# Linear-attention kernel, two layers: k's softmax chain in pieces, k'v's sums in another PSUM bank, q dealt by two engines, one output tile ahead of k'v

## The reference, cut to what matters

```
xn = layernorm(x)
q, k, v = xn @ Wq + bq, xn @ Wk + bk, xn @ Wv + bv      # k and v masked
q = softmax(q of a head, over its columns)
k = softmax(k of a head, over the 512 tokens)
att = einsum(k, v)            # per head, k'v
y = einsum(q, att)
scale, shift = silu(emb) @ W_emb + b_emb
h = layernorm(y) * (1 + scale) + shift
x = x + silu(h) @ W_out + b_out
```

## Time and profile before

| | us |
|---|---|
| median of 3 runs | 852.2 (851.95 to 852.74) |
| the profiled execution | 852.96 |
| its span | 851.2 |
| its granted TensorE clock, mean | 0.99 |
| TensorE busy | 788.6 (93%) |
| VectorE busy | 610.0 (72%) |
| ScalarE busy | 443.5 (52%) |
| GpSimd busy | 387.4 (46%) |
| DMA queue of SyncE | 42.8% of 16 engines |

### The profile page before, as it was taken

One profiled execution on the slowest core, in us unless ns is written; L12 is line 12 of the kernel. 1 busy time (PEld: TensorE's weight loads), 2 busy tenths in 40 slices (PEclk: granted clock), 3 DMA queues, 4 the chain that ended last, 5 costly groups with the idle time before them and its releaser, 6 DMA issues.

```text
span 851.2 us, 15057 instructions
## 1 busy us (share of the span) xinstructions
PE 788.6 (93%) x5307; PEld 681.6 (80%) x5307; DVE 610.0 (72%) x1277; ACT 443.5 (52%) x660; POOL 387.4 (46%) x444
## 2 busy tenths in 40 slices
PE   7987969998999999899999989999898999989997
PEld 6656758887888888788888878888787888878886
DVE  6777858768685876868587686857768685764664
ACT  6341383646547263664846366472646637273642
POOL 3040243626455262656746266452625445352462
PEclk9998979999999999999999999999999999999999
DMA  8972234343434434345483434344243434426112
GB/s 264 320 244 66 87 94 149 78 148 115 134 134 136 148 78 151 113 133 183 119 267 96 149 113 143 135 133 156 72 130 135 124 135 114 131 65 233 33 68 99
DMA packets 121687, 115.36 MB, mean 136 GB/s; under 512 B 16152, under 2 KB 106264, under 8 KB 115744
## 3 DMA queue, kind: packets, MB, share of 16 engines
q1 hardware_dynamic: 121632, 114.65, 42.8%
HBM read 51.68 MB, written 16.78 MB: 80 GB/s over the span
## 4 chain that ended last, share of the span: by engine, by line
PE 74%; DVE 17%; issue 4%; ACT 1%; SPq 1%; POOL 1%; DMA 1%; DVEq 0%; POOLq 0%; ACTq 0%
PE psum_w L489 43%; PE psum_k L489 20%; PE psum_t L581 6%; DVE q L974 3%; PE psum_k L720 3%; DVE k_top L944 2%; DVE y L987 1%; DVE k_shift_rows L962 1%; DVE y_stats L994 1%; DVE k_top L941 1%; DVE k_top L950 1%; SPq L389 1%; DVE q_max L976 1%; DVE y_moments L998 1%; DVE k_exp L801 1%
## 5 line engine op out<-in xcount | busy, mean ns | idle before, releaser
L1461 POOL TENSOR_TENSOR q<-q,q_max 128x512 f32<-128x512 f32 x64 | 67.1, 1048 | 244.6 <-DVE q_max L976 244.6
L1284 ACT ACTIVATE q<-q 128x512 f32<-128x512 f32 x64 | 40.1, 626 | 235.9 <-POOL q L1461 235.9
L489 PE MATMUL psum_w<-w_high_v,xT_high 128*128 128x512 f32 x240 | 93.0, 387 | 22.1 <-DVE q L974 22.1
L1413 POOL TENSOR_TENSOR gT_low<-yT,gT_high 128x512 fp32r<-128x512 f32 x56 | 71.8, 1285 | 69.9 <-ACT gT_high L1254 66.7
L489 PE MATMUL psum_k<-w_high_k,xT_high 128*128 128x512 f32 x240 | 93.6, 390 | 8.6 <-DVE att L1042 6.5
L1405 POOL TENSOR_TENSOR xT_low<-xT,xT_high 128x512 fp32r<-128x512 f32 x56 | 71.7, 1281 | 57.1 <-ACT xT_high L1208 53.5
L489 PE MATMUL psum_w<-w_high_q,xT_high 128*128 128x512 f32 x240 | 94.9, 395 | 0.0
L489 PE MATMUL psum_w<-w_high_o,gT_high 128*128 128x512 f32 x240 | 92.6, 386 | 0.0
L489 PE MATMUL psum_k<-w_low_k,xT_high 128*128 128x512 f32 x240 | 92.2, 384 | 0.0
L489 PE MATMUL psum_k<-w_high_k,xT_low 128*128 128x512 f32 x240 | 92.0, 383 | 0.0
L489 PE MATMUL psum_w<-w_low_v,xT_high 128*128 128x512 f32 x240 | 91.0, 379 | 0.0
(11 more groups left out here) (189 smaller groups left out, 1840.9 us busy)
## 6 DMA issues: line engine op xcount, KB each, us to landing
qT<-k_exp SPq DMA_DIRECT2D x240, 64.0 KB, 2.0
yT<-raw_weights SPq DMA_DIRECT2D x240, 64.0 KB, 2.0
xT<-raw_weights SPq DMA_DIRECT2D x224, 64.0 KB, 2.0
raw_weights<-x_between_layers SPq DMA_DIRECT2D x10, 1024.0 KB, 6.9
x_res<-in_x SPq DMA_DIRECT2D x8, 1024.0 KB, 5.0
x_between_layers<-x_res SPq DMA_DIRECT2D x8, 1024.0 KB, 4.1
raw_weights<-in_x SPq DMA_DIRECT2D x6, 1024.0 KB, 6.7
x_res<-x_between_layers SPq DMA_DIRECT2D x6, 1024.0 KB, 4.8
```

The source lines that it names most:

```text
L489: mm = pe.matmul(bank, lhs[:, c, of_tile(t)], alternating(rhs[m][:, c, :]), start=(c == 0 and n == 0), stop=(c == CHUNKS - 1 and n == 2))
L1284: act.activation(q[:, t, :], q[:, t, :], ACT.Exp).then_inc(q_exp_ready, 1)
L1413: pool.tensor_tensor(low[:, c, :], yT[:, c, :], high[:, c, :], ALU.subtract).then_inc(g_low_ready, 1)
L1461: pool.tensor_tensor(rows_q, rows_q, q_max[:, t, 0:HEADS[layer]].unsqueeze(2) .to_broadcast([P, HEADS[layer], width]), ALU.subtract).then_ ...
```

## The change

PSUM: k'v's sums go to `psum_t` bank 0, in iteration 0 to `psum_w` bank 0; K tile 0 waits for no `att_ready`, k'v waits until y of the batch before is taken.

```diff
-        def att_psum_of(layer):
-            return head_view(psum_k[:, 0, :], layer, SUMS)
+        def att_psum_of(i, layer):
+            bank = psum_w[:, 0, :] if fixed(i, 0) else psum_t[:, 0, :, :].rearrange("p c n -> p (c n)")
+            return head_view(bank, layer, SUMS)
```

```diff
                     if t == 0:
-                        pe.wait_ge(att_ready, i)
...
-                    if t >= 2:
-                        attend(i - 1, t - 2, att_layer)
+                    if t >= 1:
+                        attend(i - 1, t - 1, att_layer)
...
                     project(i, t, Q, psum_w[:, t % 2, :])
-                    if t < 2:
-                        attend(i - 1, t + 2, att_layer)
+                    if t == 0:
+                        attend(i - 1, 3, att_layer)
...
+                if gives_out(i):
+                    out_projection(i - 2, 0, v_ready, TILES * i + 3)
                 pe.wait_ge(k_exp_ready, TILES * (i + 1))
                 pe.wait_ge(v_ready, TILES * (i + 1))
                 pe.wait_ge(v_masks_ready, 2 * (i + 1))
+                if fixed(i, 0):
+                    pe.wait_ge(q_biased, 3)
+                elif fixed(i, LAST):
+                    pe.wait_ge(qT_ready, 3)
+                else:
+                    wait_apart(pe, y_ready, TILES * i)
```

VectorE: `k_shift_of` is cut into `k_top_of_halves` (L937 to L946), `k_top_of_all` (L947 to L953) and `spread_k_shift` (L954 to L963), `shift_k` takes two tiles at a time, and y is normalised here. The old order is L1099 to L1147; the new one:

```diff
+                raise_k_max(i, 0)
+                if turns_x: turn_x_blocks(i + 1, 0); turn_x_blocks(i + 1, 1)
+                raise_k_max(i, 1)
+                take_y(j, att_layer, 0)
+                if turns_x: turn_x_blocks(i + 1, 2)
+                stats_of_y(j, 0)
+                raise_k_max(i, 2)
+                take_y(j, att_layer, 1)
+                if turns_x: turn_x_blocks(i + 1, 3)
+                stats_of_y(j, 1)
+                if turns_x_late: turn_x_blocks(i + 1, t) for all t     # iteration 1
+                raise_k_max(i, 3); turn_k_max(i)
+                take_y(j, att_layer, 2); k_top_of_halves(i)
+                take_q(i, layer, 0);     k_top_of_all(i)
+                take_y(j, att_layer, 3)
+                take_q(i, layer, 1);     spread_k_shift(i, layer)
+                take_q(i, layer, 2);     shift_k(i, (0, 1))
+                take_q(i, layer, 3);     shift_k(i, (2, 3))
+                stats_of_y(j, 2); stats_of_y(j, 3)
+                moments_of_y(j, t) for all t
+                if normalises_x(i): x_stats_of(i + 2)
+                for t in range(TILES):
+                    normalise_y(j, t)
+                    turn_y_blocks(j, t)
+                if gives_out(i) and not fixed(i, LAST): add_residual(i - 2, 0)
+                turn_q_blocks(i, t) for all t
                 sum_attention(i, layer)
...
+            def normalise_y(j, t):
+                if t == 0:
+                    dve.wait_ge(y_factors_done, 2 * (j + 1))
+                dve.tensor_scalar(y[:, t, :], y[:, t, :], y_moments[:, t, 0:1], y_rstd[:, t:t + 1],
+                                  ALU.subtract, ALU.mult).then_inc(yn_ready, 1)
```

ScalarE loses `normalise_y`; exp of q tile 3 goes behind exp of k tiles 0 and 1; in iteration 1 `prepare_x(2)` goes between the masks of v; and it issues eight of q's DMAs, SyncE the other eight:

```diff
+        def deal_q(eng, i, quadrants):
+            eng.wait_ge(q_blocked, TILES * (i + 1))
+            if attends(i):
+                wait_apart(eng, y_psum, TILES * i)
+            deal(eng, qT[:, :, :, :].rearrange("p a c n -> p a (c n)"), q_blocks, q_dealt, quadrants)
...
+                    deal_q(sp, i, (2, 3))
...
                     normalise_x(i + 2)
...
+                if not fixed(i, LAST):
+                    deal_q(act, i, (0, 1))
                 act.wait_ge(table_loaded, i + 1)
                 preload_silu()
```

GpSimd: y's factors need two instructions in place of four, and the order, of all iterations, is:

```diff
-                shift_q(i, layer, 0)
-                shift_q(i, layer, 1)
+                for t in range(TILES):
+                    shift_q(i, layer, t)
+                if gives_out(i):
+                    bias_residual(i - 2, 0)
+                    bias_residual(i - 2, 1)
                 if attends(i):
                     y_factors(i - 1)
-                shift_q(i, layer, 2)
-                shift_q(i, layer, 3)
                 if gives_out(i):
-                    for t in range(TILES):
-                        bias_residual(i - 2, t)
+                    bias_residual(i - 2, 2)
+                    bias_residual(i - 2, 3)
+                if normalises_x(i):
+                    x_factors(i + 2)
                 if not fixed(i, LAST):
                     low_of_x(i + 1)
-                if normalises_x(i):
-                    x_factors(i + 2)
```

More of the change, by code:

```diff
@@ L919, in raise_k_max @@
             def raise_k_max(i, t):
+                if t == 0 and attends(i):
+                    wait_apart(dve, att_ready, i)
                 dve.wait_ge(k_psum, TILES * i + t + 1)
@@ L933, in turn_k_max, with k_top_of_halves @@
                 dve.transpose(k_turned[:, :, :].rearrange("p b r -> p (b r)"), k_max[:, :]).then_inc(k_max_turned, 1)
-            def k_shift_of(i, layer):
-                of_quad, other_half, of_half, other_quad, of_all, shift = (k_top[:, n, :] for n in range(6))
+            of_quad, other_half, of_half, other_quad, of_all, shift = (k_top[:, n, :] for n in range(6))
+            def k_top_of_halves(i):
                 steps = K_TOP_STEPS * i
@@ L1098, in iteration @@
                 j = i - 1
+                turns_x, turns_x_late = deals_x(i) and not fixed(i, 1), fixed(i, 1)
                 raise_k_max(i, 0)
-                if deals_x(i):
+                if turns_x:
                     turn_x_blocks(i + 1, 0)
@@ L1123, in iteration @@
                     moments_of_y(j, t)
-                take_q(i, layer, 2)
-                k_shift_of(i, layer)
-                take_q(i, layer, 3)
-                for t in range(TILES):
-                    turn_y_blocks(j, t)
-                shift_k(i)
                 if normalises_x(i):
                     x_stats_of(i + 2)
+                for t in range(TILES):
+                    normalise_y(j, t)
+                    turn_y_blocks(j, t)
+                if gives_out(i) and not fixed(i, LAST):
+                    add_residual(i - 2, 0)
                 if not fixed(i, LAST):
@@ L1134, in iteration @@
                         turn_q_blocks(i, t)
-                if gives_out(i) and not fixed(i, LAST):
-                    add_residual(i - 2, 0)
                 sum_attention(i, layer)
@@ L1289, in copy_last_q @@
                          psum_t[:, t % 2, :, :].rearrange("p c s -> p (c s)")).then_inc(qT_ready, 1)
-            def normalise_y(j):
-                act.wait_ge(y_factors_done, 4 * (j + 1))
-                for t in range(TILES):
-                    act.activation(y[:, t, :], y[:, t, :], ACT.Identity, scale=y_rstd[:, t:t + 1],
-                                   bias=y_offset[:, t:t + 1]).then_inc(y_normed, 1)
             def normalise_x(i):
@@ L1349, in iteration @@
                     copy_last_q(2)
[L1350 to L1351 removed]
+                if fixed(i, 1):
+                    prepare_x(2, 0, (2,))
                 mask_v(i, layer, 3)
@@ L1354, in iteration @@
                     copy_last_q(3)
+                elif fixed(i, 1):
+                    prepare_x(2, 0, (3,))
                 else:
```

130 lines of the change are left out of this document (70 added, 60 removed).

## The result

The changed kernel takes 829.6 us (median of 4 runs, 827.62 to 830.04), the kernel before beside it 852.5: a ratio of 0.972, 95% interval 0.970 to 0.975. The profiled execution took 827.62 with a span of 825.8, the fastest of the four; before it was 852.96 and 851.2. So the two traces differ by 25.4 us, the medians by 22.9. In what follows every number of one kernel is from its one profiled execution, and medians are named.

What follows compares the result with a forecast made beforehand. TensorE was taken to set the time, its waiting to be what can be won. Middle -33.9, start -0.5 and end +4.0 sum to -30.4 us: 821.8 against the median of 852.2, range 812 to 835.

Steps and rivals of the forecast that it cites:

- the likeliest case: The forecast itself, whole kernel: 821.8 us, own range 816 to 828, chance 0.61.
- The middle: End of iteration 2's attends to K tile 0 of iteration 15: 39.1 us of waits and restarts fall to 5.2, -33.9.
- The chain in pieces: k's shift chain on VectorE, split between takes of y and q: V tile 1's wait goes, 1.6 us to spare.
- output tile 0: Put ahead of k'v on TensorE: its 2.59 us cover V tile 3's mask and exp of k; k'v's wait goes.
- VectorE's late stretch: VectorE's work after q tile 3, through y's normalisations and transposes: ends at 38.5, before k'v's end at 39.1.
- The normalisation: y's normalisation, moved to VectorE after x's statistics: 1.0 us each, bounds 0.45 and 1.3.
- the first rival: VectorE's late stretch replaces the wait; output tile 3 or A1 waits 0.5 to 1.2 us per iteration: 834 us, chance 0.18.
- the third rival: DMA issues of ScalarE and SyncE slow each other, y's deal ends 5.1 us later: 867 us, chance 0.06.
- The loop in it: y's landing, A1, Q3, y's transposes, next landing: 45.7 us, hidden under TensorE's 46.9; 50.8 if the deal is stretched.
- The start: Up to attend 3 and Q1 of iteration 2: ends at about 139.7 for 140.2, -0.5 us, between -4 and +4.
- The end: From K tile 0 of iteration 15: y's transposes end later, delaying the last gate and add; +4.0 us, between 1 and 6.
- The -1.0 and +0.6: Terms of the end: 1.0 us off for GpSimd's former waits for VectorE, 0.6 added for lower clock after a wait.

Runs made afterwards that it cites:

- the kernel before with this part alone: Against the kernel before: exp(q)'s transfers dealt by two engines, ScalarE tiles 0 and 1, SyncE tiles 2 and 3; 857.7 us, ratio 1.007.

## Why the prediction was right or wrong

The forecast was 821.8 and the result 829.6: inside the range of 812 to 835, outside the 816 to 828 of the likeliest case. In the terms of the profiled executions 30.4 us less were forecast, and 25.3 were found. Of the other 2.7 us, 2.0 are that the profiled run after was the fastest of its four, and 0.7 that the one before stood that much above its median.

**The middle: -33.9 forecast, -34.4 found.** The chain in pieces and output tile 0 work as forecast: undone they cost 19.2 and 12.7 us of the twelve iterations, and output tile 0 with its add gives 10.6 when done alone. Undoing the new bank or the normalisation on VectorE costs the middle 3.5 and 4.2, little above the spread, and leaves the steady periods within 0.1 us of the changed kernel's. The size is right by luck: two errors cancel. I kept 0.4 us an iteration for slips; there are none, and the periods are 46.47 and 47.25, exactly the work (16 products, four attends and k'v). That is 5 us better. Against it iterations 7 and 8, the change of layers, take 97.3 for 93.7, which I did not look at; no row of mine was from there. (Rows of the kernel before would not have shown it: its iterations 7 and 8 take 49.4 and 50.0, as their neighbours.) There GpSimd makes the low part of weights beside k's chain. Of the changed kernel, GpSimd's timeline in iteration 7 and VectorE's:

```profile
369.09 4.98 POOL L1466 TENSOR_TENSOR w_low_k<-raw_weights,w_high_k 128x512 fp32r<-128x512 f32 x4 [1.74 <-ACT w_high_k L1227]
```

```profile
371.67 1.20 DVE L964 COPY k_top<-k_top 64x16 f32<-64x16 f32 x1
372.90 1.20 DVE L966 TENSOR_TENSOR k_top<-k_top 128x16 f32<-128x16 f32 x1
```

**The account of the three parts was incomplete.** I gave output tile 0 no other condition than its own bank's. That its add had to go ahead of q's transposes is in the diff, and I took it for a detail; without it three quarters of this part are lost (2.8 for 10.6). The same add is missing from the sum for VectorE's late stretch: it takes 0.65 us between y's last transpose, forecast for 38.5, and k'v's end at 39.1, so that the cover of 0.6 was none by my own numbers.

**The normalisation: 1.0 us taken, 0.80 measured** (60 of them, from 0.50 to 1.6). The one at 341.78 takes 1.26 beside a GpSimd instruction on the residual's bias, two later ones 0.51. y's transposes end at 38.0 for 38.5. That the normalisations are shorter than assumed, 0.8 us for the four, makes up for the add that I left out: VectorE is through 0.16 ahead of k'v's end. So the first rival was close, and that it did not come true is in part luck.

**Two issuers: the third rival was wrong.** The median issue takes 0.63 us on ScalarE (0.60 to 1.18) and 0.60 on SyncE (0.59 to 1.85), which is SyncE's median in the kernel before too; the median landing is 2.0 to 2.1 us on both. The loop in it was right in kind, and it is what the kernel with all of q on SyncE falls into. That ScalarE would have 27% of the span to spare is a slip: 443.5 us busy and 15 times 5.1 of 851.2 leave 39%. Nothing hung on it.

**The start: -0.5 forecast, +2.7 found.** The mechanism I named came as forecast: GpSimd's low part at 69.4 (69.2), K tile 0 at 71.1 (70.5). What failed is the term for iteration 2. y's deal landed 2 us later than my 124.5, and I had put no price on the clock behind attend 1's wait. The changed kernel's windows of 129 to 132 and 132 to 136 (busy of PE, PEld, DVE, ACT, POOL, then clock, DMA share, GB/s):

```profile
129.00:132.00 3.00, 2.56 (x10) 2.50 (x11) 2.57 (x6) 2.94 (x5) 2.80 (x3) 0.50 0.33 85
132.00:136.00 4.00, 4.00 (x14) 3.27 (x14) 1.80 (x4) 1.29 (x2) 1.27 (x1) 0.62 0.17 44
```

Attend 1 takes 2.10 - 1.06 = 1.0 us more than one at full clock, K tile 3 there 4.38 for 2.59. The start also spreads: K tile 0 of iteration 1 was at 71.1 to 73.0 in the seven kernels whose iteration 0 is nearly or wholly that of the changed one, and at 65.2 to 67.0 in the four of the old kind. The two traces that I compare are the earliest of either kind, so the 3.2 us that separate forecast and trace are uncertain by 2 us either way.

**The end: +4.0 forecast, +6.4 found.** The path is the forecast one, and the term mis-sized is the 4.4 for y's transposes: they end 37.7 after K tile 0 (36.1), 6.1 later than before. The forecast let the factors wait for two `bias_residual`, but named no time for the factors themselves. They take 1.3 us (767.66 to 769.01 on GpSimd), and VectorE waits until then. The -1.0 and +0.6 I can't tell apart in the trace. This is VectorE's first normalisation in iteration 15, and SyncE's deal behind it:

```profile
769.04 1.50 DVE L809 TENSOR_SCALAR y<-y,y_moments,y_rstd 128x512 f32<-128x512 f32 x1 [2.24 <-POOL y_rstd L1435]
```

```profile
775.10 10.71 SPq L331 DMA_DIRECT2D yT<-raw_weights  x16
```

GpSimd's queue holds the first normalisation of the last batch, too:

```profile
796.30 1.48 DVE L1074 TENSOR_SCALAR y<-y,y_moments,y_rstd 128x512 f32<-128x512 f32 x1 [8.69 <-POOL y_rstd L1514]
```

**The marks** that I had named: no wait of V tile 1 (none; in iteration 7 0.85 ahead of a Q tile and 0.34 ahead of V tile 0), k'v right behind output tile 0 (yes), periods 46.9 and 47.5 (46.5 and 47.25), `low_of_x(1)` near 69 (yes), the last y 4.4 later (6.1).

## What to carry to other kernels

When a wait is taken out by doing work earlier, follow the buffer that this work fills to whoever must empty it: the wait returns there if its reader stands behind an unrelated wait. A chain of transfers through one issuer is a loop; compare its period with the work's before shortening anything else. Price the first and the last iteration by themselves: here a change that gained 34 us in the middle lost 9 at the two ends, and mending those, by order and by one more deal on two engines, gave 20 by the medians and 15 by the traces.

## What was not expected of the hardware

The text at the start says that each engine runs its instructions in the program's order. ScalarE's DMA issues did not wait for the arithmetic ahead of them in its program. In iteration 6 its first q transfer is issued at 350.90 while three of four x normalisations, which come first in the program, begin later. From the changed kernel's timeline of ScalarE:

```profile
350.45 0.81 ACT L1336 ACTIVATE raw_weights<-raw_weights,x_offset,x_rstd 128x512 f32<-128x512 f32 x1
350.90 0.61 ACTq L331 DMA_DIRECT2D qT<-k_exp  x1
351.17 0.80 ACT L1336 ACTIVATE raw_weights<-raw_weights,x_offset,x_rstd 128x512 f32<-128x512 f32 x1
351.54 0.62 ACTq L331 DMA_DIRECT2D qT<-k_exp  x1
```

I had q's issues begin 44.0 us after K tile 0; they begin at 41.4. The other way round they did wait. In the kernel before with this part alone, the cast that follows eight issues starts only as the last is out (68.94), and in every iteration of the changed kernel but the last, which has no such issues, ScalarE's table load starts only behind the last of them (356.43 in iteration 6, after 3.06 us idle). So in these traces arithmetic waits for issues ahead of it, and issues do not wait for the last few arithmetic instructions ahead, up to five of which were still to start.
